# A router in the shadow of attention, one slot shorter

## The reference

```python
h = _layernorm(x) * (1 + ca) + sa
x = x + ga * attention(h)             # one head, 512 keys, width 128
h = _layernorm(x) * (1 + cb) + sb
x = x + gb * _L1_ffn_ref(h)           # 8 experts, the best 2 per row

def _L1_ffn_ref(tgt):
    logits = einsum('bsd,ed->bse', tgt, Wr) + br
    top_v, top_i = top_k(logits, 2)
    top_w = softmax(top_v)
    o = relu(tgt @ W1[e] + b1[e]) @ W2[e] + b2[e]   # per expert, inner width 512
    return layer_norm(tgt + sum of the two o weighted by top_w)
```

## The kernel before

| step of group q | engine | slot |
|---|---|---|
| power -1/2 of the variances, `rs_b` (line 1292), waits for `b_mv` of slot E | POOL | E |
| normalised rows `xn_b` (line 1520) | DVE | E + 1 |
| transposes, `hidden_rows` (line 1720), and `h4` (line 1366) | PE, ACT | E + 2 |
| rows and logits (line 1727), copies `row` (lines 1375, 1376), `eexp` (line 1372) | PE, ACT | E + 3 |
| logits, two largest, their places, masks `mk`, `ms`, sums `base`, weights (lines 1527 to 1551) | DVE | E + 3 |
| ranks within an expert (lines 1737, 1739) | PE | E + 4 |
| ranks read (line 1481), times the masks, places `pos` (line 1492, semaphore `q_pos`) | DVE | E + 5, ahead of `x` of that slot |
| four sends, two for each chunk (line 1268), wait for `q_pos`, and for `x` of the slot before (`x_new`) | POOL | E + 5 |

## Time and profile before

### The profile page before, as it was taken

The page is one execution under the profiler, slowest core; times in us unless marked ns, Lnnn a source line. Parts: engine busy times, 40 slices in busy tenths (PEclk is TensorE's granted clock), DMA queues, the critical chain, the costliest instruction groups (busy, mean ns, idle before and its releaser), DMA issues.

```text
span 571.1 us, 12107 instructions
## 1 busy us (share of the span) xinstructions
PE 508.1 (89%) x3328; PEld 421.1 (74%) x3328; DVE 434.1 (76%) x1603; ACT 351.3 (62%) x944; POOL 280.1 (49%) x355
## 2 busy tenths in 40 slices
PE   4799999999999999888999999724999999999990
PEld 3477888888888888756777766614999999999630
DVE  3757898989898989977899988883667666666275
ACT  3978687877878585445566555412666666555354
POOL 2133453635353536510166666772667666666323
PEclk9979999999999999999999999856999999999996
DMA  8299999999400000005511111112222222222293
GB/s 271 75 300 175 170 162 172 175 154 176 112 20 1 19 19 2 20 20 190 153 44 40 39 38 35 48 54 59 62 72 71 68 73 68 64 70 67 82 279 111
DMA packets 76385, 54.69 MB, mean 96 GB/s; under 512 B 10524, under 2 KB 69408, under 8 KB 76184
## 3 DMA queue, kind: packets, MB, share of 16 engines
q1 hardware_dynamic: 70352, 43.39, 39.5%
q0 software_dynamic: 4320, 8.99, 4.7%
q10 hardware_dynamic: 1640, 1.45, 0.8%
HBM read 40.62 MB, written 31.58 MB: 126 GB/s over the span
## 4 chain that ended last, share of the span: by engine, by line
PE 72%; DVE 11%; ACT 7%; issue 4%; DMA 3%; POOL 1%; SPq 0%; another core or an unknown queue 0%; DVEq 0%; ACTq 0%; POOLq 0%
PE bank L1819 12%; PE bank L1836 11%; PE bank L681 5%; PE bank L683 5%; PE bank L682 5%; PE bank L792 4%; PE bank L1712 4%; PE bank L1695 3%; PE bank L727 2%; PE bank L812 2%; PE bank L1701 2%; PE bank L738 2%; PE bank L788 2%; PE bank L797 2%; PE bank L723 1%
## 5 line engine op out<-in xcount | busy, mean ns | idle before, releaser
L1312 POOL DMA_INDIRECT results<-arena x71 | 74.9, 1055 | 55.4 <-ACT arena L1400 50.8
L1819 PE MATMUL bank<-front,arena 128*128 128x128 f32 x568 | 77.4, 280 | 1.7 <-ACT front L1394 0.6
L1268 POOL DMA_INDIRECT queue<-arena,pos x64 | 62.6, 978 | 31.4 <-issue 14.2
L1836 PE MATMUL bank<-h_all,front 128*128 x568 | 75.7, 276 | 0.1
L1819 PEld LDWEIGHTS bank<-front,arena 128*128 128x128 f32 x568 | 70.2, 195 | 4.3 <-issue 3.8
L296 POOL TENSOR_TENSOR arena<-arena,half_neg 128x1 f32<-128x1 f32 x32 | 18.7, 584 | 111.2 <-ACT arena L462 111.2
L1836 PEld LDWEIGHTS bank<-h_all,front 128*128 128x128 f32 x568 | 69.1, 192 | 0.4 <-issue 0.3
L1609 DVE COPY arena<-arena 128x516 f32 x71 | 36.0, 507 | 40.9 <-issue 38.9
L1394 ACT ACTIVATE front<-bank 128x128 f32<-128x128 f32 x71 | 19.7, 277 | 58.3 <-PE bank L1812 40.6
L681 PE MATMUL bank<-h_hi,wc_hi 128*128 128x512 f32 x96 | 45.0, 469 | 1.3 <-ACT arena L443 1.3
L1620 DVE TENSOR_SCALAR front<-bank,arena 128x128 f32<-128x128 f32 x142 | 42.8, 343 | 3.8 <-PE bank L1819 3.7
(11 more groups left out here) (299 smaller groups left out, 1390.0 us busy)
## 6 DMA issues: line engine op xcount, KB each, us to landing
queue<-in_pad_rows SPq DMA_DIRECT2D x8, 2178.0 KB, 34.5
arena<-queue SPq DMA_DIRECT2D x71, 66.0 KB
rows<-mod_rows SPq DMA_DIRECT2D x8, 384.0 KB, 6.6
x_keep<-x SPq DMA_DIRECT2D x8, 256.0 KB, 2.2
arena<-in_w SPq DMA_DIRECT2D x1, 2048.0 KB, 9.0
h_all<-in_w SPq DMA_DIRECT2D x1, 2048.0 KB, 8.0
h_all<-results SPq DMA_DIRECT2D x8, 256.0 KB, 4.8
arena<-results SPq DMA_DIRECT2D x8, 256.0 KB, 5.0
```

Of the source, the lines that this page charges most:

```text
L1268: pool.indirect_dma_start(k.queue, bass.IndirectOffsetOnAxis(ap=pos[:, s, i, c0 + j:c0 + j + 1], axis=0), row[:, s * NC + c0 + j, i, :], N ...
L1312: pool.indirect_dma_start(k.results, bass.IndirectOffsetOnAxis(ap=xg[:, c, D:D + 1].bitcast(I32), axis=0), yw[:, c, :], None).then_inc(S[f ...
L1819: mm = t_.matmul(bank[(2 if g < NG // 2 else 6) + p][:, g * P:g * P + P], wc[:, p, g * P:g * P + P], xt[:, p, :], start=True, stop=True)
L1836: mm = t_.matmul(bank[4 + p][:, 0:D], ht[:, p, g * P:g * P + P], w2[:, e, g, :], start=(g == 0), stop=(g == NG - 1))
```

## The change

In attention's router: VectorE no longer writes the normalised rows; it forms minus mean times `rs_b` (`nm_b`) in slot E + 1 right behind the maxima, and ACT writes the rows at the end of its slot E + 1. Rows and logits move to slot E + 2, behind the transposes on PE. VectorE finds the two largest logits and their places in slot E + 2; masks, sums and weights stay in slot E + 3. Ranks go to slot E + 3, `pos` to slot E + 4. The sends stand in slot E + 3, without the wait for `x_new`, and in a slot that held both they would follow the power. END falls to NT + 5. A query product also waits for its bank. In the mixer, `ve1` and its instruction are gone: a constant in the statistics is changed to match, and the power reads the variances that `bn_aggr` wrote.

```diff
@@ statistics of the mixer
-            g_.memset(st1[:, :, 8:9], P * (EPS + 0.5))
+            g_.memset(st1[:, :, 8:9], P * EPS)
-                    wait(pool, "l1_ve", g + 1)
+                    wait(pool, "l1_ag", NC * (g + 1))
-                    g_.tensor_tensor(rs1[:], ve1[:], half_neg[:], ALU.pow).then_inc(S["l1_rs"], 1)
+                    g_.tensor_tensor(rs1[:], mv1[:].rearrange("p c t -> p (c t)")[:, 1::2], half_neg[:], ALU.pow).then_inc(S["l1_rs"], 1)
-                if norm and norm[-1] == NC - 1:
-                    wait(dve, "l1_ag", NC * (gl + 1))
-                    v.tensor_scalar(ve1[:], mv1[:].rearrange("p c t -> p (c t)")[:, 1::2], 0.5, None, ALU.subtract).then_inc(S["l1_ve"], 1)
@@ slots
-                at = max(at + (1.0 if n == NC else 0.75), end_of[q] + 5)
+                at = max(at + 0.75, end_of[q] + 3)
-        BEGIN, END = -9, NT + 6
+        BEGIN, END = -9, NT + 5
@@ GpSimd
-                for q, j in scatters_at.get(m, ()):
-                    if chunk(m):
-                        wait(pool, "x_new", m)
-                    scatter(q, j)
                 if m in ends_at:
...
                     g.tensor_tensor(rs_b[:, 0:n], mv_b[:, s % 2, c0:c0 + n].rearrange("p c t -> p (c t)")[:, 1::2], k.half_neg[:, 0:n], ALU.pow).then_inc(S["b_rs"], 1)
+                for q, j in scatters_at.get(m, ()):
+                    scatter(q, j)
@@ ScalarE: slot m begins with eexp (m - 3), copies row after h4 (m - 2), and ends with
+                if m - 1 in ends_at:
+                    q = ends_at[m - 1]
...
+                    wait(act, "b_nm", q + 1)
+                    for i in range(n):
+                        ins = ac.activation(xn_b[:, i, :], x[:, s * NC + c0 + i, :], ACT.Identity, scale=rs_b[:, i:i + 1], bias=nm_b[:, i:i + 1])
+                    ins.then_inc(S["b_xn"], 1)
@@ VectorE, behind the maxima nmx
-                if m - 5 in ends_at:
-                    q = ends_at[m - 5]
+                if m - 1 in ends_at:
+                    q = ends_at[m - 1]
+                    s, c0, n = groups[q]
+                    wait(dve, "b_rs", q + 1)
+                    v.scalar_tensor_tensor(out=nm_b[:, 0:n], in0=mv_b[:, s % 2, c0:c0 + n].rearrange("p c t -> p (c t)")[:, 0::2], scalar=-1.0, in1=rs_b[:, 0:n],
+                                           op0=ALU.mult, op1=ALU.mult).then_inc(S["b_nm"], 1)
+                if m - 3 in ends_at:
...
+                        v.tensor_tensor(mk[:, q % 2, i, 0:n], top_i[:, 0:n, i:i + 1].broadcast_to([P, n, NE]), over_chunks(k.iota[:], n), ALU.is_equal).then_inc(S["q_mask"], 1)
...
+                if m - 4 in ends_at:
+                    q = ends_at[m - 4]
                     s, c0, n = groups[q]
                     filled(dve, ("rank", q))
@@ VectorE, behind the statistics
-                if m - 1 in ends_at:
...
-                        ins = v.tensor_scalar(xn_b[:, i, :], x[:, s * NC + c0 + i, :], mv_b[:, s % 2, c0 + i, 0:1], rs_b[:, i:i + 1], ALU.subtract, ALU.mult)
-                if m - 3 in ends_at:
-                    q = ends_at[m - 3]
+                if m - 2 in ends_at:
+                    q = ends_at[m - 2]
...
+                if m - 3 in ends_at:
+                    q = ends_at[m - 3]
...
                     wait(dve, "q_exp", q + 1)
@@ TensorE
             def query(s, first):
...
+                bank_free(pe, ("q", s))
@@ order in a slot: turn_p, scores, hidden_rows, attend, value, query, key, rows_and_logits, ranks
+                if m - 2 in ends_at:
+                    hidden_rows(ends_at[m - 2])
                 if chunk(m):
                     attend(m)
...
                 if m - 2 in ends_at:
-                    hidden_rows(ends_at[m - 2])
+                    rows_and_logits(ends_at[m - 2])
                 if m - 3 in ends_at:
-                    rows_and_logits(ends_at[m - 3])
-                if m - 4 in ends_at:
-                    ranks(ends_at[m - 4])
+                    ranks(ends_at[m - 3])
```

More of the change, by code:

```diff
@@ L1040, in layer1 @@
         st_a = sb("st_a", [P, NC, 6]); mv_a = sb("mv_a", [P, NC, 2]); ve_a = sb("ve_a", [P, NC]); rs_a = sb("rs_a", [P, NC])
-        st_b = sb("st_b", [P, 2, 9]); mv_b = sb("mv_b", [P, 2, NC, 2]); rs_b = sb("rs_b", [P, NC])
+        st_b = sb("st_b", [P, 2, 9]); mv_b = sb("mv_b", [P, 2, NC, 2]); rs_b = sb("rs_b", [P, NC]); nm_b = sb("nm_b", [P, NC])
         front = k.front
@@ L1154, in layer1 @@
             if m - 2 in ends_at:
-                used(("h4", ends_at[m - 2]), "u_act")
+                used(("row", ends_at[m - 2]), "u_act")
             if m - 3 in ends_at:
-                used(("row", ends_at[m - 3]), "u_act")
-            if m - 4 in ends_at:
-                used(("rank", ends_at[m - 4]), "u_dve")
+                used(("rank", ends_at[m - 3]), "u_dve")
             if m == 2:
@@ L1339, in body @@
                     ac.activation(eexp[:, 0:1], ones[:, 0:1], ACT.Exp)
+                if m - 3 in ends_at:
+                    q = ends_at[m - 3]
+                    n = groups[q][2]
+                    wait(act, "q_diff", q + 1)
+                    wait(act, "q_w1", q)
+                    ac.activation(eexp[:, 0:n], ediff[:, 0:n], ACT.Exp).then_inc(S["q_exp"], 1)
                 n = m + 1
@@ L1343, in body @@
                     ac.activation(pt[:, n % 3, :], bank[5][:], ACT.Copy).then_inc(S["p_act"], 1)
+                if m - 2 in ends_at:
+                    q = ends_at[m - 2]
+                    s, _, n = groups[q]
+                    filled(act, ("h4", q))
+                    if q >= 2:
+                        filled(act, ("row", q - 2))
+                    elif first:
+                        wait(act, "s_yz", NT)
+                    ac.activation(h4[:, q % 2, 0:n * P], bank_of(("h4", q))[:, 0:n * P], ACT.Identity, scale=mod[:, 1, 4, s:s + 1], bias=mod[:, 1, 3, s:s + 1]).then_inc(S["u_act"], 1)
+                if m - 3 in ends_at:
+                    q = ends_at[m - 3]
+                    s, c0, n = groups[q]
+                    src = rows_in(q, n)[:, :, 0:P]
+                    ac.activation(row[:, s * NC + c0:s * NC + c0 + n, 0, 0:D], src, ACT.Copy)
+                    ac.activation(row[:, s * NC + c0:s * NC + c0 + n, 1, 0:D], src, ACT.Copy).then_inc(S["u_act"], 1)
                 n = m + 3
@@ L1357, in body @@
                     ac.activation(kT[:, s % 2, :], bank_of(("k", s))[:], ACT.Identity, bias=k.attn_b[:, 1:2]).then_inc(S["u_act"], 1)
[L1358 to L1366, removed]
-                if m - 3 in ends_at:
-                    q = ends_at[m - 3]
-                    s, c0, n = groups[q]
[L1370 to L1376, removed]
+                if m - 1 in ends_at:
+                    q = ends_at[m - 1]
+                    s, c0, n = groups[q]
+                    if q >= 1:
+                        filled(act, ("h4", q - 1))
+                    wait(act, "b_nm", q + 1)
+                    for i in range(n):
+                        ins = ac.activation(xn_b[:, i, :], x[:, s * NC + c0 + i, :], ACT.Identity, scale=rs_b[:, i:i + 1], bias=nm_b[:, i:i + 1])
+                    ins.then_inc(S["b_xn"], 1)
             merged(mixer_of["scalar"](act), body)
@@ L1476, in body @@
                     v.tensor_reduce(nmx[:, n % 2:n % 2 + 1], bank[3 + n % 2][:], AX.X, ALU.max, negate=True).then_inc(S["sc_max"], 1)
-                if m - 5 in ends_at:
-                    q = ends_at[m - 5]
+                if m - 1 in ends_at:
+                    q = ends_at[m - 1]
+                    s, c0, n = groups[q]
+                    wait(dve, "b_rs", q + 1)
+                    v.scalar_tensor_tensor(out=nm_b[:, 0:n], in0=mv_b[:, s % 2, c0:c0 + n].rearrange("p c t -> p (c t)")[:, 0::2], scalar=-1.0, in1=rs_b[:, 0:n],
+                                           op0=ALU.mult, op1=ALU.mult).then_inc(S["b_nm"], 1)
+                if m - 3 in ends_at:
+                    q = ends_at[m - 3]
+                    s, c0, n = groups[q]
+                    at, done = s * NC + c0, s * NC + c0 + n
+                    wait(dve, "q_at", done)
+                    for i in range(2):
+                        v.tensor_tensor(mk[:, q % 2, i, 0:n], top_i[:, 0:n, i:i + 1].broadcast_to([P, n, NE]), over_chunks(k.iota[:], n), ALU.is_equal).then_inc(S["q_mask"], 1)
+                    wait(dve, "q_mask", 2 * (q + 1))
+                    v.tensor_tensor(ms[:, 0:n], mk[:, q % 2, 0, 0:n], mk[:, q % 2, 1, 0:n], ALU.add).then_inc(S["q_ms"], 1)
+                    wait(dve, "q_ms", q + 1)
+                    if q == 0:
+                        wait(dve, "a_set", 1)
+                    for i in range(n):
+                        wait(dve, "q_base", at + i)
+                        v.tensor_tensor(base[:, q % 2, i + 1, :] if i + 1 < n else base[:, (q + 1) % 2, 0, :], base[:, q % 2, i, :], ms[:, i, :], ALU.add).then_inc(S["q_base"], 1)
+                if m - 4 in ends_at:
+                    q = ends_at[m - 4]
                     s, c0, n = groups[q]
```

(7 more changed lines are left out.)

22 lines of the change are left out of this document (12 added, 10 removed).

## The result

The changed kernel takes 617.7 us (median of 4 runs, 616.27 to 619.29) against 567.28 us of the kernel before (566.41 to 567.84). The ratio is 1.088 (95% interval 1.0855 to 1.0909): slower by 50.4 us. The forecast was 618 us, range 603 to 641, with 0.92 on slower.

A forecast was written before the change was run, and what follows sets the result against it. Before, no engine had 3 us to spare per pair; the change would close a loop through sends and power. Loop +40.2, start +4.6, tail -3.7, clock +10: +51 us, from 567.2 to 618 us, range 603 to 641.

The forecast's parts named there:

- The loop: Attention: `pos`, four sends, power, `nm_b`, rest of DVE's slot, next `pos`; 13 pairs at 130.6 against 90.4 us, +40.2.
- the sum: Loop: thirteen pairs with additions, gatings and last slots, 130.6 us; whole forecast: all terms with the clock, +51 us.
- plain pair: Attention: a pair of slots, 5.99 us from `pos` to `nm_b` plus 3.72 of DVE's work and 0.03, 9.74 us.
- value additions and gatings: In the loop's own part: a value addition of 0.68 in five pairs, two gatings of 0.30 in four, +5.8 us.
- Start and tail: Power of group 2 at 286.5, not 281.91, +4.6 us; eight sends, not twelve, behind the last power, -3.7 us.
- The clock: PE in attention, idle in every pair, falls to half clock and scores come late; bounds 0 and 19, taken +10 us.
- Rival B: Slower still: PE stays at half clock and its 12.6 us bind the pair instead of 9.74; 645 us, chance 0.08.
- the mixer's part: Mixer: the subtraction, 8 of 0.158 us, goes; worth nothing under busy PE, -1.3 us without that cover.
- ScalarE's rows and TensorE's new order: Attention: ACT's two more rows of work a group, and the transposes waiting for them, come later than the loop's steps; nothing.
- rival A: Faster: sends run through before the power is wanted, no loop closes, only the tail's 3.7 us remain; 563.5 us, chance 0.06.
- The exchange of power and sends: POOL's list within a slot: does nothing, since powers are in odd slots and sends in even ones.

## Why the prediction was right

**The loop.** Right in its place and its members: `pos`, four sends, power, `nm_b` at the head of the slot, and VectorE's work. Each member was measured as priced: 0.28 for 0.29 us to the first send, 0.02 to the power, 0.03 to its reader. Shorter by two sends, shorter by VectorE's work behind the wait, and opened, it gave pairs of 7.20, 8.23 and 7.66 us. Its size was a little too long: at a clock of 0.99 thirteen pairs took 127.0 us, where the sum has 130.6. A plain pair took 9.60 us for 9.74, and the value additions and gatings 3.6 us for 5.8.

**Start and tail** were right to 0.2 us against the recorded profile of before, the eight sends behind the last power included.

**The clock** was oversized: +10 us was taken, and it cost 7.4 us in the pairs of the first trace and 4.5 us in those of the second. The mechanism was the one described, late scores ahead of the maxima, but it cost nothing in every second pair: in five of these seven the granted clock was 0.98 or more, and in the last two (0.81 and 0.52 in the first trace) the fall missed the path. Loop and clock were both put too high: together they were forecast at 140.6 us for the 13 pairs, and took 134.3 and 131.5. Rival B, a TensorE at half clock throughout, is ruled out by the pairs with a granted clock of 1.00.

**What the sum was taken from.** The difference of 50.4 us was met by +51 by luck. Between the two profiles from which the sum was worked out and is to be judged, the difference is 45.7 us, 5.4 us less than the sum's 51.1. The medians differ by more, because the base differed. On the 566.8 us chip the kernel with only the mixer's part, which times like before, has its 13 pairs in 86.4 us (6.65 a pair, 366.36 - 279.97), not 90.4, and the changed kernel 131.5: +45.1, with +6.7 at the start (forecast 4.6), -3.3 in the tail and +0.7 behind it, 49.2 us in all. A hit within 1 us is more exact than the steps deserve.

**A step that was wrong without showing.** ScalarE's rows and TensorE's new order were costed at nothing, under the loop's waits. Under the loop no cost of theirs shows: its pairs at full clock are as long as the loop's own sum, or shorter. But they are not free: each alone costs 0.6 to 0.9%, and the kernel in which the loop is open loses 1.6 to 1.8%, of which they are the likely part. The same goes for rival A: it put the time at 563.5 us if no loop closed, and the kernel in which none closes is slower than before. Its ratio of 1.016 to 1.018 would be 576 to 578 us. The rival had the right condition and the wrong price, because it took the other engines' new order for harmless; VectorE's share in that was not tried.

**The exchange of power and sends** does nothing, as stated: only a slot's difference between the two puts the power ahead, and then it is worth seven per cent.

**The mixer's part**: nothing, as costed.

## What to carry to other kernels

When an instruction that waits is moved earlier in one engine's list without its input coming earlier, look at what stands behind it in that list and who reads that, and add up the ring; a send of 1.27 us that was hidden becomes part of the period. A slot number orders lists, not times: the sends stood in a slot before the one in which their places were formed. And a change that sits under a larger wait shows no cost of its own; take the large wait away before calling the rest free.

## What was not expected of the hardware

The same kernel took 566.8, 572.5 and 574.1 us on three chips, each over ten or more runs within 0.4% of their median. Between the traces, the pairs of slots of attention differ, 6.65 us on the fastest with the mixer's part only, 6.87 and 6.96 us in two profiles of before. Why one chip is slower stayed open.

On GpSimd the first send of a group, but for group 0, starts 0.27 to 0.30 us behind its `pos` where the list has no wait for `x_new` ahead of it. In the kernel before with its sends early, which has that wait, it starts 0.78 or 0.79 us behind, though the wait had been met before. If the wait is the cause, which no run tried alone, the change is half a microsecond a loop better off than early sends in the kernel before.
